# Experts stage of a two-layer transformer: gates applied to the outputs, and the choice of experts placed beside their products

## The reference, cut to what matters

```
h = layernorm(x) * gain + shift                     # adaptive norm of the layer
logit[t, e] = -|h[t] - keys[e]|^2 + h[t] . rw[e] + rb[e]
gates = softmax over the 4 largest logits of a token, 0 elsewhere
y[t] = sum over e of gates[t, e] * (w2[e] @ gelu(w1[e] @ h[t] + b1[e]) + b2[e])
x = x + gate_mod * y
```

## Time and profile before

| | us |
|---|---|
| median of 3 runs | 2741.39 (2740.1 to 2742.93) |
| profiled execution | 2747.67 |
| its span | 2745.9 |
| norm ahead of the experts | 370.4 to 384.6 |
| experts, until the next norm's first transpose | 384.6 to 820.2 |
| windowed layers | from about 950 to the end |

### The profile page before, as it was taken

How to read it: one execution, slowest core, us unless ns; L and a number is a source line. 1 busy time by engine, 2 the same in 40 slices (tenths; PEclk the granted TensorE clock), 3 DMA queues, 4 the chain that set the end, 5 groups by cost and what they waited for, 6 DMA issues and landing times. The chain is left out here.

```text
span 2745.9 us, 60937 instructions
## 1 busy us (share of the span) xinstructions
PE 2496.5 (91%) x22102; PEld 1616.5 (59%) x22102; DVE 2259.3 (82%) x4840; ACT 1623.9 (59%) x2742; POOL 1429.5 (52%) x1184
## 2 busy tenths in 40 slices
PE   6699658999997579999999999999999999999996
PEld 3377445777764335666566666666666656665662
DVE  2488546777775689999999999999999999999982
ACT  2133126888873246666666666666666666666662
POOL 0000004777760167666666666666666666666650
PEclk8799868999997699999999999999999999999996
DMA  1000010000000111111111111111111111111110
GB/s 65 4 7 4 8 39 9 24 23 23 23 8 1 54 37 30 31 30 53 42 30 31 53 43 33 30 53 25 46 29 50 30 46 31 30 30 40 35 27 19
DMA packets 45776, 84.31 MB, mean 31 GB/s; under 512 B 13397, under 2 KB 27205, under 8 KB 44360
## 3 DMA queue, kind: packets, MB, share of 16 engines
q1 hardware_dynamic: 45512, 80.76, 10.9%
HBM read 32.50 MB, written 1.05 MB: 12 GB/s over the span
## 5 line engine op out<-in xcount | busy, mean ns | idle before, releaser
L1527 PE MATMUL w_psP<-w_qkv,w_xs 128*128 128x512 f32 x1152 | 606.8, 610 | 41.5 <-DVE w_bb L1652 28.1
L1727 POOL TENSOR_TENSOR w_ab<-w_ab,w_bb 128x512 f32<-128x512 f32 x384 | 486.5, 1275 | 172.4 <-DVE w_bb L1652 172.4
L1732 POOL TENSOR_TENSOR w_ab<-w_ab,w_nrm 128x512 f32<-128x512 f32 x384 | 396.1, 1046 | 112.3 <-DVE w_nrm L67 112.3
L1737 POOL TENSOR_TENSOR w_pb<-w_pb,w_sm 128x768 f32<-128x768 f32 x192 | 282.6, 1472 | 302.5 <-DVE w_sm L1680 302.5
L1592 ACT ACTIVATE w_sq<-w_psP 128x512 f32<-128x512 f32 x384 | 229.4, 597 | 225.9 <-PE w_psP L1527 157.5
L1011 POOL TENSOR_TENSOR e_glo<-e_hg,e_ghi 128x512 fp32r<-128x512 f32 x192 | 272.3, 1449 | 153.9 <-ACT e_ghi L990 153.9
L1651 DVE TENSOR_TENSOR w_ab<-w_psP,w_tabs 128x512 f32<-128x512 f32 x384 | 262.3, 683 | 27.3 <-ACT w_sq L1592 11.7
L1533 PEld LDWEIGHTS w_psT<-tables_all,w_ab 128*128 128x128 f32 x1536 | 179.7, 141 | 169.9 <-issue 117.9
L1620 ACT ACTIVATE w_pT<-w_psA 128x512 f32<-128x512 f32 (+1 forms) x384 | 227.6, 593 | 65.4 <-PE w_psO L1576 44.4
L1652 DVE TENSOR_TENSOR w_bb<-w_psP,w_tabs 128x512 f32<-128x512 f32 x384 | 261.2, 680 | 0.0
L1658 DVE TENSOR_REDUCE w_nrm<-w_sq 128x8 f32<-128x512 f32 x384 | 254.3, 673 | 1.3 <-ACT w_sq L1592 1.3
(11 more groups left out here) (292 smaller groups left out, 5012.3 us busy)
## 6 DMA issues: line engine op xcount, KB each, us to landing
w_v_even<-tables_layer SPq DMA_DIRECT2D x72, 256.0 KB, 3.1
w_qkv<-in_w_qkv SPq DMA_DIRECT2D x6, 1536.0 KB, 7.4
w_v_even<-tables_layer SPq DMA_DIRECT2D x72, 128.0 KB, 3.0
e_raw<-in_w_moe SPq DMA_DIRECT2D x32, 256.0 KB, 2.7
w_v_even<-w_v SPq DMA_DIRECT2D x24, 256.0 KB, 3.2
w_xs<-H SPq DMA_DIRECT2D x168, 32.0 KB, 1.9
w_o<-in_w_o SPq DMA_DIRECT2D x6, 512.0 KB, 3.8
w_xsf<-H SPq DMA_DIRECT2D x24, 128.0 KB, 2.2
```

What stands on the lines that cost most here:

```text
L1527: pe.matmul(psP[u % 2][:, :], xs[:, 128 * k:128 * (k + 1)], w_qkv[:, ds(layer % 2, 1), 512 * at:512 * at + 512], start=True, stop=True).th ...
L1727: pool.tensor_tensor(a, a, bb[:, i % 2, :], ALU.add).then_inc(s["ad"], 1)
L1732: pool.tensor_tensor(a, a, nrm[k // 2][:, 1, 8 * (i % 8):8 * (i % 8) + 8].unsqueeze(2).to_broadcast([128, 8, DH]), ALU.mult).then_inc(s["n ...
L1737: pool.tensor_tensor(p, p, sm[k % 2][:, :].unsqueeze(2).to_broadcast([128, PAIRS, KEYS]), ALU.mult).then_inc(s["pn"], 1)
```

## The change

- The gates no longer multiply the hidden values. ScalarE rounds the GELU's output itself, VectorE makes all four rests, and GpSimd has no part in the units. Each unit's output has its own accumulation in psY (start at j = 0), and VectorE computes (psY + b2) * gate into `tmp` and adds that to an SBUF sum `acc` (`weigh`, `add`), two units behind.
- The gates reach all partitions by DMA: transposed gates (16 experts by 512 tokens in each quarter of the partitions) are written to a DRAM tensor `gate_rows`, and for each expert one transfer reads its row of 2048 values into all 128 partitions of `gb` (two buffers).
- The logits are computed with experts in partitions: for each batch 32 output columns, four batches side by side on TensorE, 512 tokens wide; then four transposes. Their constant is added as a column.
- The choice is cut in `order_experts` and `choose_experts`, which VectorE runs after its rests of units 0 and 1; TensorE runs hidden(0) before the logits, transposes to tokens after hidden(1), and back to experts after outputs(2).
- Four psH banks. Splitting of H goes by batch. b1, b2 and the router's bias come in one tensor. The squares of H are GpSimd's.
- The stage's first loads are issued by SyncE at the start of the norm ahead (`adaln(c, 0, 1, loads)` inside `experts`).
- No hardware loops: the 64 units are written out.

```diff
 @sync
+    sp.wait_ge(s["gT"], 1)
+    for b in range(NB):
+        sp.dma_start(rows[:, 0, at(b)], gT[32 * b:32 * b + E, :]).then_inc(s["rows"], 16)
+    sp.wait_ge(s["rows"], 16 * NB)
+    for e in range(E):
+        if e >= 2:
+            sp.wait_ge(s["wlo"], e - 1)
+            load_weights(sp, e)
+            sp.wait_ge(s["ev"], (e - 1) * NB)
+        sp.dma_start(gb[e % 2][:, :], rows[e].to_broadcast([128, T])).then_inc(s[f"gb{e % 2}"], 16)
 @tensor
-                    if j == 1:
-                        wait(pe, s["hg"], (n - 1) * C)
-                        pe.matmul(psR[b % 2][:, :], sel[u][:, :], gT3[:, b * N:(b + 1) * N], start=True,
-                                  stop=True).then_inc(s["g"], 1)
+            def outputs(n):
+                e, b = n // NB, n % NB
+                wait(pe, s["ev"], n - 3)
+                for j in range(C):
+                    pe.wait_ge(s["glo"], n * C + j + 1)
...
+            def logits():
+                pe.wait_ge(s["k"], 1)
+                pe.matmul(psY[3][:, 0:16], ksq[:, :, :].rearrange("p b e -> p (b e)"), nones[:, 0:16], ...)
+                for b in range(NB):
+                    pe.matmul(psY[2][32 * b:32 * b + 32, :], kr[:, b, :], c.H[:, at(b)], start=True, stop=False,
+                              skip_group_check=True)
+                pe.wait_ge(s["hsq"], NB)
+                for b in range(NB):
+                    last = pe.matmul(psY[2][32 * b:32 * b + 32, :], nones[:, :], hsq[:, at(b)], ...)
+                last.then_inc(s["l"], 1)
...
+            hidden(0)
+            logits()
+            for n in range(1, UNITS):
+                hidden(n)
+                if n == 1:
+                    by_tokens()
+                if n == 4:
+                    pe.wait_ge(s["gT"], 1)
+                outputs(n - 1)
+                if n == 3:
+                    by_experts()
+            outputs(UNITS - 1)
 @scalar
+                gelu(n, 0)
+                gelu(n, 1)
+                round_hidden(n, 0)
+                gelu(n, 2)
+                round_hidden(n, 1)
+                gelu(n, 3)
+                round_hidden(n, 2)
+                round_hidden(n, 3)
 @vector
+            def weigh(n):
+                e, b = n // NB, n % NB
+                dve.wait_ge(s["y"], n + 1)
+                dve.wait_ge(s[f"gb{e % 2}"], (e // 2 + 1) * 16)
+                wait(dve, s["acc"], n - 5)
+                dve.scalar_tensor_tensor(out=acc[:, at(b)] if e == 0 else tmp[b % 2][:, :], in0=psY[b][:, :], scalar=b2(e),
+                                         in1=gb[e % 2][:, at(b)], op0=ALU.add, op1=ALU.mult).then_inc(s["ev"], 1)
...
+            WEIGHED = {4: (0, 1), 5: (2, 3), 6: (4,), 7: (5,)}
+            for n in range(UNITS):
+                if n < 8:
+                    for j in range(C):
+                        rest(n, j)
+                    for m in WEIGHED.get(n, ()):
+                        weigh(m)
+                        add(m)
+                else:
+                    rest(n, 0)
+                    weigh(n - 2)
+                    rest(n, 1)
+                    add(n - 2)
+                    rest(n, 2)
+                    rest(n, 3)
+                if n < 2:
+                    split_hidden(n + 2)
+                if n == 0:
+                    order_experts()
+                elif n == 1:
+                    choose_experts()
+                elif n == 3:
+                    dve.wait_ge(s["gt"], 1)
+                    dve.tensor_copy(gT[:, :], psY[3][:, :]).then_inc(s["gT"], 1)
+                if n % NB == 2 and n // NB < E - 1:
+                    split_weights(n // NB + 1)
```

More of the change, by code:

```diff
@@ L261, in _, with adaln @@
             ch.link(dve.tensor_copy(c.band_bf[:, :, :], c.band[:, :, :]))
-def adaln(c, layer, part):
+def adaln(c, layer, part, loads=None):
     nc, n = c.nc, f"n{layer}{part}_"
@@ L280, in adaln, with _ @@
     with nc.Block() as block:
+        if loads is not None:
+            @block.sync
+            def _(sp):
+                loads(sp)
         @block.tensor
@@ L853, in experts @@
+    with ExitStack() as inner:
+        outer, c.stage = c.stage, inner
+        adaln(c, 0, 1, loads)
+        c.stage = outer
+    psH = [c.ps(f"e_psH{j}") for j in range(C)]
     psY = [c.ps(f"e_psY{b}") for b in range(NB)]
[L854 to L857, removed]
@@ L882, in _ @@
         def _(pe):
[L884 to L912, removed]
             def split_product(out, hi, lo, mov_hi, mov_lo, start, stop):
@@ L944, in expert_pair @@
[L944 to L955, removed]
@@ new lines, in by_tokens, with by_experts @@
+            def by_tokens():
+                pe.wait_ge(s["lgT"], 1)
+                for t in range(TILES):
+                    tt = slice(128 * t, 128 * t + 128)
+                    last = pe.transpose(psY[3][:, tt], lgT[:, tt], c.ident[:, :])
+                last.then_inc(s["lt"], 1)
+            def by_experts():
+                pe.wait_ge(s["gate"], 1)
+                for t in range(TILES):
+                    last = pe.transpose(psY[3][:, 128 * t:128 * t + 128],
+                                        gate3[:, t * NB:(t + 1) * NB, :].rearrange("p b e -> p (b e)"), c.ident[:, :])
+                last.then_inc(s["gt"], 1)
@@ L965, in split_weights @@
-            def split_weights(u, e):
-                act.wait_ge(s[f"we{u}"], (e // 2 + 1) * 48)
-                wait(act, s["y"], (e - 1) * NB)
[L968 to L974, removed]
-                act.activation(gT[b % 2][:, :], psR[b % 2][0:ROWS, :], ACT.Copy)
-                act.activation(gT3[:, b * N:(b + 1) * N], psR[b % 2][0:ROWS, :], ACT.Copy).then_inc(s["gTe"], 1)
@@ L1095, in _, with split_hidden @@
[L1095 to L1102 removed]
+            def split_hidden(b):
+                dve.wait_ge(s["hhi"], b + 1)
+                dve.tensor_tensor(Hlo[:, at(b)], c.H[:, at(b)], Hhi[:, at(b)], ALU.subtract).then_inc(s["hlo"], 1)
@@ new lines, in split_weights, with rest @@
+            def split_weights(e):
+                dve.wait_ge(s["whi"], e + 1)
+                dve.tensor_tensor(wlo[e % 2][:, :, :], raw[e % 2][:, :, :], whi[e % 2][:, :, :],
+                                  ALU.subtract).then_inc(s["wlo"], 1)
+            def rest(n, j):
+                b = n % NB
+                dve.wait_ge(s["ghi"], n * C + j + 1)
+                dve.tensor_tensor(glo[b % 2][:, j, :], hh[b % 2][:, j, :], ghi[b % 2][:, j, :],
+                                  ALU.subtract).then_inc(s["glo"], 1)
@@ new lines, in result, with order_experts @@
+            def result(b):
+                dve.wait_ge(s["acc"], (E - 2) * NB + b + 1)
+                dve.scalar_tensor_tensor(out=c.X[:, at(b)], in0=acc[:, at(b)], scalar=c.mods[:, 0, 5, b:b + 1],
+                                         in1=c.X[:, at(b)], op0=ALU.mult, op1=ALU.add)
+            def order_experts():
+                dve.wait_ge(s["lt"], 1)
+                ch.link(dve.tensor_copy(lg[:, :, :], psY[3][:, :].rearrange("p (k e) -> p k e", e=32)[:, :, 0:E]))
+                for t in range(NT):
+                    m = ch.inc(dve.max(m8[:, t, :], lg[:, t, :]))
+                ch.wait(m)
+                ch.inc(dve.tensor_tensor(gt[:, :, :], lg[:, :, :], kth, ALU.is_gt))
+                ch.link(dve.tensor_tensor(eq[:, :, :], lg[:, :, :], kth, ALU.is_equal))
+                dve.tensor_tensor(lg[:, :, :], lg[:, :, :], m8[:, :, 0].unsqueeze(2).to_broadcast([128, NT, E]),
+                                  ALU.subtract).then_inc(s["lg"], 1)
+                ch.link(dve.tensor_reduce(left[:, :], gt[:, :, :], AX_X, ALU.add))
+                ch.link(dve.tensor_scalar(left[:, :], left[:, :], -1.0, float(TOPK), ALU.mult, ALU.add))
@@ L1105, in causal_attention @@
+            result(0)
+            weigh(UNITS - 2)
+            result(1)
+            add(UNITS - 2)
+            weigh(UNITS - 1)
+            result(2)
+            add(UNITS - 1)
+            result(3)
 def causal_attention(c):
```

283 lines of the change are left out of this document (113 added, 170 removed).

## The result

The new kernel takes 2680.43 us in the median of 4 runs (2679.08 to 2685.72), the old one 2742.16 (4 runs, 2740.1 to 2743.39): ratio 0.9779, interval 0.9762 to 0.9796. 2683 was forecast. In a later session the same kernel took 2693.32 us beside 2743.59 (ratio 0.9815, 0.9788 to 0.9841); that difference is taken up with the last experiments. One later run of the old kernel took 4782.3 us, unexplained, and no ratio here counts it. The profiled execution has a span of 2678.5 us against 2745.9.

A forecast was written before the change was run, and what follows sets the result against it. TensorE's queue was taken to set the pace of the expert units, behind a 45.7 us start. Gains 41.0 (first product) + 19.9 (products) - 2.3 (end) = 58.6 us, from 2741.4 to 2682.8, forecast 2683; range 2671 to 2700.

The forecast's parts named there:

- First product: Stage start to first expert product: 4.7 us instead of 45.7, a gain of 41.0 (38 to 43).
- Units: 64 steady expert-by-batch units at TensorE's pace: 24 matmuls of 0.231, 5.54 us each instead of 6.04, 354.6 us in all.
- The split of the 0.50 us a unit: In the old unit of 6.04 us, all time beyond 24 matmuls (5.54) was put on the gate broadcast matmul.
- Room of the other engines: In steady units ScalarE (nearer 4.6 us, 5.50 by whole durations) and VectorE (4.5) stay under TensorE's 5.54.
- the first rival: VectorE's subtract costs 1.55 us even without GpSimd, so VectorE paces units at 7.93 us: 2835 us; 2%.
- ScalarE takes over: ScalarE needs 5.98 us a unit, so nothing is won in the units: 28 us less gain, 2711 us; 6%.
- What comes back: Work returning to TensorE among products: half clock 2.3, logits 3.3, transposes 1.2, choosing 1.3, DRAM stall 6.1; sum 14.2 us.
- half clock: The 12 matmuls of hidden(0) run at 1.2 GHz: 5.1 us instead of 2.8, +2.3.
- choosing: VectorE's choice of experts between subtracts of units 0 to 2 makes products of unit 1 or 2 wait 1.3 us (0 to 4).
- DRAM: Gates' way through DRAM ends the first weighing at 46.5 us; TensorE, wanting the bank at 40.4, stalls 6.1 (0 to 13).
- the broadcast sets the pace: Gate broadcasts from one DRAM row beyond 22.2 us each pace the experts; at 30 us, 2823; 3% slower, 2% no change.
- End: Last matmul to next stage: weigh, add and result follow on VectorE, 3.6 us instead of 1.3, a loss of 2.3.

The follow-up runs named there:

- the last experiments: Five small moves at the stage's start and end, against the new kernel timed beside it: 2680.24 us where the new kernel took 2693.32.
- the version with the squares moved away: New kernel with five small moves, among them GpSimd's squares behind the first split of weights: 2683.81 us (0.9803), then 2680.24 (0.9768).
- the GpSimd experiment: New kernel plus three unused GpSimd squares of 512 columns of H in every unit from unit 4 on: 2708.12 us, ratio 0.9878 to the old kernel.
- the second profile: New kernel unchanged, profiled again in a later session beside the version with five small moves: median 2693.32 us, stage 376.7 us.

## Why the prediction was right, and what of it was not

*First product:* 4.2 us against 4.7. Right, and by the means named: the weights wait for nothing, and both subtracts pay the price beside GpSimd, as the version with the squares moved away confirms (2.9).

*Units:* 5.60 against 5.54, 64 of them: 3.8 us too low. A third of that is arithmetic: 3.94 us for 17 steps is 0.232, not 0.231. The old kernel's same 17 steps are 0.232 in the mean of all units of 440 to 740 us; the new kernel's are 0.2335, and stay so with GpSimd busy, with two banks, and with twice the broadcast traffic. What makes them longer is not shown.

**The split of the 0.50 us a unit is the step that failed, and its larger error is hidden in a right sum.** I wrote that it belonged to the broadcast, "its own step of 0.23, and the two steps behind it take 0.71 instead of 0.46", and that the waits for the GELU lay "most of it under other matmuls". The broadcast removed alone gained nothing (1.0001); put back alone into the new kernel, the bank wait costs 0.41 and the broadcast 0.23. The wait for the GELU was the limit (95 waits of weight loads, 21.6 us or 0.34 a unit), and the broadcast filled part of the same gap. Had the change removed only the matmul, the same working would have promised 64 x 0.50 = 32 us, and it brings none. The sum came right because the change removed both.

*Room of the other engines:* VectorE 216 of 300 us, ScalarE 260, no stall in units 8 to 63. The subtract at 0.69 was right to the hundredth; the first rival is out by the trace, and the GpSimd experiment brings its price back, 1.52 for a subtract that starts beside GpSimd. The rival "ScalarE takes over" is out: 5.50 us of whole durations did not turn into a pace; ScalarE is busy for 4.85 us a unit (4.6 forecast).

*What comes back:* half clock 2.35 (2.3), logits 391.42 to 393.49, 2.07 (3.3: they ran at full clock), transposes 0.7 by the starts of the matmuls (1.2, for which no row was named), choosing 0.9 (1.3), DRAM 2.6 (6.1). Together 8.6 against 14.2. (The products take 368.0 us, and 64 units of 5.60 leave 9.6 of them; the last 1.0 are the longer steps around each interruption.) That error of some 5 us has the other sign than the 3.8 of the units, and that the two cancel is luck.

In the stall, the mis-sized terms are mainly the DMAs: the writes were issued at 33.0 us after the stage's start (34.7 by my sum) and landed in 1.7 (2.6), the broadcast in 4.8 from its issue at 35.9 (6.7 from 38.8), so the weighing was over at 41.5 instead of 46.5, while the bank was wanted at 38.8 (40.4). The rival "the broadcast sets the pace" is out: the 16 land in 4.3 to 6.8 us, one is needed each 22.4, and twice the traffic slows no unit.

*End:* from the last matmul's step (754.28) to the next stage 3.9 us against 3.6.

*The stage:* 59.5 us less against 58.6, and 58.9 in the second profile (376.7). The forecast gave its length before as 435.3; its own rows give 435.6.

*Outside the stage:* 7.9 us between the profiled executions, booked at nothing. Behind the stage the 5.4 lie in attention and its norms, where the same code ran at another clock: 0.68 in the old kernel's profile over the 140 us of the line below, 0.71 in the new one's over 760 to 900.

```profile
822.10:962.10 140.00, 90.03 (x326) 55.87 (x326) 83.76 (x231) 41.33 (x87) 9.56 (x16) 0.68 0.08 27
```

The later profile of the new kernel shows that it can be 15 us the other way behind the stage. The forecast was within 3 us of the first median and some 10 of the later one: both in the range. The nearness to 2683 is partly chance; the stage's 59.5 is what the working is to be judged by.

## What to carry over

When a matmul stands next to a short wait of the same engine, removing the matmul may only uncover the wait: ask, for every instruction taken out, when its successor's inputs and bank would be ready without it, and count the pair as one cost. Two partial undoings, one per cause, show in one look whether causes add or overlap. A stall can cost more than its length: ask what the clock does behind it, and give the sum a term for it. The duration of a VectorE instruction with two SBUF inputs holds only for what GpSimd does beside it, so taking work off GpSimd can pay on VectorE.

## What was not expected of the hardware

- A 1 MB broadcast of one 8 KB DRAM row to 128 partitions lands in 4.7 us (median of 16, 4.3 to 6.8). The one load of 1 MB of separate rows in the old kernel took 6.3, but with other loads beside it, so which is faster is not shown. With two in a row the second landed 6.9 us after its issue (median).
- After a stall of TensorE of 2.2 to 2.6 us the granted clock stayed at 1.00 in two executions and fell to half for 7 to 9 steps in three (1.5 us more); two of the five are the same kernel, one of each kind. After 4.7 us it was half at once, for 13 steps. After 1.1 to 1.2 us it stayed at 1.00, twice.
- Beside a busy GpSimd a VectorE subtract with two SBUF inputs takes 0.68, 0.86 or 1.52 us, by when it meets the other; one with an input from PSUM stayed at 0.74.
- A step of 128 x 512 is 0.232 us in the old kernel and 0.2335 in the new one, with the same matmuls; the cause is open.
